# Attention heads: GpSimd splits the last key tile of the transposed exponentials, ScalarE copies it in fp32, and the output sum is made in place

## What is computed

```
x = x + L0_ffn(L0_cond(x))          # an oscillator stepped through time, then a gated MLP with a Hadamard mix
Q, K, V = Wq x, Wk x, Wv x          # per batch b of 8: 16 heads of 16 channels, 512 positions
att = (Q^T K) / sqrt(16) + b0
att = att * m + (1 - m) * -1e30     # m: one mask value per key
att = softmax(att)                  # over 512 keys
y = att V                           # per head 512 x 16
x = x + L1_ffn(y)                   # 8 experts, the top 2 of each position
```

## Time and profile before

| | us |
|---|---|
| median of 3 runs (3069.7 to 3072.78) | 3070.81 |
| the profiled execution | 3071.74 |
| its span | 3070.0 |
| PE busy (41104 matmuls) | 2550.0, 83% |
| DVE busy | 2533.3, 83% |
| ACT busy | 1217.3, 40% |
| POOL busy | 1352.2, 44% |

### The profile page before, as it was taken

One profiled execution on the slowest core, in us unless ns is written; L12 is line 12 of the kernel. 1 busy time (PEld: TensorE's weight loads), 2 busy tenths in 40 slices (PEclk: granted clock), 3 DMA queues, 4 the chain that ended last, 5 costly groups with the idle time before them and its releaser, 6 DMA issues. The chain is left out here.

```text
span 3070.0 us, 116365 instructions
## 1 busy us (share of the span) xinstructions
PE 2550.0 (83%) x41104; PEld 1785.2 (58%) x41104; DVE 2533.3 (83%) x11914; ACT 1217.3 (40%) x4102; POOL 1352.2 (44%) x3951
## 2 busy tenths in 40 slices
PE   4478888888888888888888778888888876999999
PEld 4356666666666666666667446555655552444444
DVE  7989999999999999999997579989999976544545
ACT  3343333333333333333333368778877760000000
POOL 6846566656666566655563323334333335000000
PEclk6599999999999999999999889999999998999999
DMA  4100000000000000000000431110111110000000
GB/s 180 42 19 10 4 10 10 10 3 10 10 10 10 3 10 10 10 7 7 10 10 10 178 91 34 46 47 25 38 47 43 37 63 8 10 17 27 0 27 14
DMA packets 43922, 88.98 MB, mean 29 GB/s; under 512 B 7168, under 2 KB 23808, under 8 KB 41600
## 3 DMA queue, kind: packets, MB, share of 16 engines
q1 hardware_dynamic: 36336, 63.11, 6.4%
q10 hardware_dynamic: 4752, 10.49, 0.9%
q0 software_dynamic: 2304, 8.39, 0.8%
HBM read 65.18 MB, written 16.78 MB: 27 GB/s over the span
## 5 line engine op out<-in xcount | busy, mean ns | idle before, releaser
L228 PE MATMUL rest<-Tl,CW 128*128 128x56 f16 x16384 | 618.1, 190 | 315.4 <-DVE Tl L494 314.9
L228 PEld LDWEIGHTS rest<-Tl,CW 128*128 128x128 f16 x16384 | 502.6, 97 | 561.2 <-DVE Tl L494 557.5
L347 ACT ACTIVATE Tf<-X 128x32 f32<-128x32 f32 x768 | 176.2, 229 | 779.2 <-DVE X L538 779.2
L1114 DVE CUSTOM_DVE_ANT_0 negL<-Lps,negC 128x512 f32<-128x512 f32 x512 | 339.7, 682 | 43.9 <-PE Lps L1022 42.7
L1032 PE MATMUL Tps<-idS,Pr 128*128 128x128 f32 x2048 | 292.3, 288 | 93.9 <-ACT Pr L1084 87.9
L1134 DVE TENSOR_TENSOR PT<-Tps,PT 128x512 f16<-128x512 f32 x512 | 348.4, 681 | 22.8 <-ACT PT L1091 21.2
L1084 ACT ACTIVATE Pr<-negL,nM 128x512 f32<-128x512 f32 x512 | 358.2, 729 | 17.2 <-DVE nM L1114 16.9
L1091 ACT ACTIVATE PT<-Tps 128x512 f16<-128x512 f32 x512 | 293.0, 597 | 139.9 <-PE Tps L1032 139.8
L625 POOL TENSOR_TENSOR G<-X,Dr 128x32 f32<-128x32 f32 x768 | 207.1, 270 | 300.2 <-DVE X L499 273.2
L1032 PEld LDWEIGHTS Tps<-idS,Pr 128*128 128x128 f32 x2048 | 229.9, 145 | 185.1 <-DVE PT L1134 131.5
L217 PE MATMUL main<-Th,CW 128*128 128x56 f16 x8224 | 264.2, 189 | 10.3 <-DVE CW L450 10.3
(11 more groups left out here) (133 smaller groups left out, 5159.1 us busy)
## 6 DMA issues: line engine op xcount, KB each, us to landing
stage<-w_up SPq DMA_DIRECT2D x8, 1024.0 KB, 4.6
qk<-qkp ACTq DMA_DIRECT2D x32, 256.0 KB, 2.4
QR<-qk SPq DMA_DIRECT2D x128, 64.0 KB, 2.2
KR<-qk SPq DMA_DIRECT2D x128, 64.0 KB, 3.2
wstage<-moe_up POOLq DMA_DIRECT2D x16, 512.0 KB, 5.6
W2m<-w_down SPq DMA_DIRECT2D x1, 4096.0 KB, 13.4
stage<-x_tb SPq DMA_DIRECT2D x16, 256.0 KB, 2.6
x<-stage SPq DMA_DIRECT2D x16, 256.0 KB, 2.1
```

Of the source, the lines that this page charges most:

```text
L228: last = pe.matmul(rest[:, m], CW[:, 0, k, m * P:(m + 1) * P], Tl[:, k:k + 1, :].to_broadcast([P, REP, B]), start=(m == 0 and k == 0), sto ...
L1114: dve.tensor_tensor_reduce(out=negL[:, qt, :], in0=Lps[qt % 2][:, :], in1=negC[:], scale=1.0, scalar=3.0e38, op0=ALU.add, op1=ALU.min, acc ...
```

## The change

Of the four key tiles, three are treated as before. For tile 3 (`KD`), ScalarE copies `Tps[3]` in fp32 into a new buffer `last_f` (two deep, by head), and GpSimd makes both halves from it in a new function `split_last`: a copy into the high half and a subtract into the low half. `split_last` of head h-1 stands in GpSimd's step behind `split_output` of head h-3. VectorE has three low halves to make per head instead of four, and its row sums now stand ahead of the last of them. TensorE's transposes of tile 3 wait for ScalarE's copy (`s_cp`) of the head before, its values wait also for GpSimd (`s_pl`), and ScalarE's copy of tile 3 waits for the split of two heads ago. Apart from that the buffer `yf` is gone: `split_output` writes its sum over the first part in `yn`, and the normalization waits for the sum of a head one later than before.

```diff
--- before.py
+++ after.py
@@ -854,8 +854,8 @@
         Pr = sb("Pr", [P, 2, DC, D])
         PT = sb("PT", [P, 2, 2, DC, D], F16)
         yn = sb("yn", [P, 4, DC, 2 * DH])
-        yf = sb("yf", [P, DC, DH])
         wstage = sb("wstage", [P, 2, 1024])
+        last_f = sb("last_f", [P, 2, D])
         Lps = [ctx.enter_context(nc.psum_tensor(f"Lps{i}", [P, 512], F32)) for i in range(2)]
         Tps = [ctx.enter_context(nc.psum_tensor(f"Tps{i}", [P, 512], F32)) for i in range(4)]
         Ops = [ctx.enter_context(nc.psum_tensor(f"Ops{i}", [P, DC, 128], F32)) for i in range(2)]
@@ -865,12 +865,14 @@
             sem("s_L"), sem("s_neg"), sem("s_exp"), sem("s_T"), sem("s_hi"), sem("s_lo"), sem("s_pv"),
             sem("s_norm"), sem("s_y"), sem("s_ri"))
         s_yh, in_moe, moe_t, moe_hi, moe_lo = sem("s_yh"), [sem("in_moe0"), sem("in_moe1")], sem("moe_t"), sem("moe_hi"), sem("moe_lo")
+        s_cp, s_ph, s_pl = sem("s_cp"), sem("s_ph"), sem("s_pl")
         halt = sem("halt2")
         block = ctx.enter_context(nc.Block())
 
 
         AHEAD = 8
         COPIES = 3
+        KD = DC - 1
 
         def load_qk(sp, b, half):
 
@@ -924,6 +926,7 @@
         @block.gpsimd
         def _(pool):
             pool.sem_inc(s_y, AHEAD)
+            pool.sem_inc(s_pl, AHEAD)
             pool.wait_ge(in_id, 32)
             pool.sem_inc(halt, 1)
 
@@ -975,17 +978,29 @@
 
                 i = b * NH + h
                 cols = slice(h * DH, (h + 1) * DH)
+                yf = yn[:, h % 4, :, 0:DH]
                 pool.wait_ge(s_norm, i + 1 + AHEAD)
                 pool.sem_inc(halt, 1)
-                pool.tensor_tensor(yf[:], yn[:, h % 4, :, 0:DH], yn[:, h % 4, :, DH:2 * DH], ALU.add).then_inc(s_y, 1)
+                pool.tensor_tensor(yf, yf, yn[:, h % 4, :, DH:2 * DH], ALU.add).then_inc(s_y, 1)
                 pool.wait_ge(s_y, i + 1 + AHEAD)
                 pool.sem_inc(halt, 1)
-                pool.tensor_copy(YH[:, b, :, cols], yf[:]).then_inc(s_yh, 1)
+                pool.tensor_copy(YH[:, b, :, cols], yf).then_inc(s_yh, 1)
                 pool.wait_ge(s_yh, 2 * i + 1)
                 pool.sem_inc(halt, 1)
-                pool.tensor_tensor(YL[:, b, :, cols], yf[:], YH[:, b, :, cols], ALU.subtract).then_inc(s_yh, 1)
+                pool.tensor_tensor(YL[:, b, :, cols], yf, YH[:, b, :, cols], ALU.subtract).then_inc(s_yh, 1)
                 pool.wait_ge(s_yh, 2 * i + 2)
                 pool.sem_inc(halt, 1)
+
+            def split_last(b, h):
+
+                i = b * NH + h
+                pool.wait_ge(s_cp, i + 1 + AHEAD)
+                pool.sem_inc(halt, 1)
+                pool.tensor_copy(PT[:, h % 2, 0, KD, :], last_f[:, h % 2]).then_inc(s_ph, 1)
+                pool.wait_ge(s_ph, i + 1)
+                pool.sem_inc(halt, 1)
+                pool.tensor_tensor(PT[:, h % 2, 1, KD, :], last_f[:, h % 2], PT[:, h % 2, 0, KD, :],
+                                   ALU.subtract).then_inc(s_pl, 1)
 
             def step(b, h):
                 real = exists(b, h, 0)
@@ -995,6 +1010,8 @@
                     load_weights(b)
                 if exists(b, h, 3):
                     split_output(*before(b, h, 3))
+                if exists(b, h, 1):
+                    split_last(*before(b, h, 1))
                 if not real:
                     return
                 if h in (4, 8):
@@ -1027,14 +1044,18 @@
                 if kc == 0:
                     pe.wait_ge(s_exp, i * DC + DC + AHEAD)
 
-                pe.wait_ge(s_lo, DC * i + kc - DC + 1 + AHEAD)
+                if kc < KD:
+                    pe.wait_ge(s_lo, KD * i + kc - KD + 1 + AHEAD)
+                else:
+                    pe.wait_ge(s_cp, i + AHEAD)
                 for qt in range(DC):
                     last = pe.transpose(Tps[kc][:, qt * P:(qt + 1) * P], Pr[:, h % 2, qt, kc * P:(kc + 1) * P], idS[:])
                 last.then_inc(s_T, 1)
 
             def values(b, h):
                 i = b * NH + h
-                pe.wait_ge(s_lo, DC * i + DC + AHEAD)
+                pe.wait_ge(s_lo, KD * i + KD + AHEAD)
+                pe.wait_ge(s_pl, i + 1 + AHEAD)
                 pe.wait_ge(s_norm, i - 1 + AHEAD)
                 for qt in range(DC):
 
@@ -1074,6 +1095,7 @@
         def _(act):
             act.sem_inc(s_exp, AHEAD)
             act.sem_inc(s_hi, AHEAD)
+            act.sem_inc(s_cp, AHEAD)
 
             def exps(b, h, qt):
                 i = b * NH + h
@@ -1088,7 +1110,11 @@
                 i = b * NH + h
                 act.wait_ge(s_T, i * DC + kc + 1 + AHEAD)
                 act.wait_ge(s_pv, i - 1 + AHEAD)
-                act.activation(PT[:, h % 2, 0, kc, :], Tps[kc][:, :], ACT.Copy).then_inc(s_hi, 1)
+                if kc < KD:
+                    act.activation(PT[:, h % 2, 0, kc, :], Tps[kc][:, :], ACT.Copy).then_inc(s_hi, 1)
+                else:
+                    act.wait_ge(s_pl, i - 1 + AHEAD)
+                    act.activation(last_f[:, h % 2], Tps[kc][:, :], ACT.Copy).then_inc(s_cp, 1)
 
             def step(b, h):
                 for qt, kcs in ((0, (0, 1)), (1, (2,)), (2, (3,)), (3, ())):
@@ -1123,26 +1149,26 @@
 
             def normalize(b, h):
                 i = b * NH + h
-                dve.wait_ge(s_y, i - 3 + AHEAD)
+                dve.wait_ge(s_y, i - 2 + AHEAD)
                 dve.wait_ge(s_ri, i + 1)
                 dve.tensor_tensor(yn[:, h % 4], Ops[h % 2][:, :, 0:2 * DH],
                                   ri[:].unsqueeze(2).to_broadcast([P, DC, 2 * DH]), ALU.mult).then_inc(s_norm, 1)
 
             def transposed_low(b, h, kc):
 
-                dve.wait_ge(s_hi, (b * NH + h) * DC + kc + 1 + AHEAD)
+                dve.wait_ge(s_hi, (b * NH + h) * KD + kc + 1 + AHEAD)
                 dve.tensor_tensor(PT[:, h % 2, 1, kc, :], Tps[kc][:, :], PT[:, h % 2, 0, kc, :], ALU.subtract).then_inc(s_lo, 1)
 
             def step(b, h):
                 if h == 0 and exists(b, h, 0):
                     dve.wait_ge(negc_ok, b + 2)
                     dve.sem_inc(halt, 1)
-                for qt, kcs in ((0, ()), (1, (0,)), (2, (1,)), (3, (2, 3))):
+                for qt, kcs in ((0, ()), (1, (0,)), (2, (1,)), (3, (2,))):
                     if exists(b, h, 0):
                         negate_and_max(b, h, qt)
+                    if qt == DC - 1 and exists(b, h, 2):
+                        invert_sums(*before(b, h, 2))
                     for kc in kcs:
-                        if kc == DC - 1 and exists(b, h, 2):
-                            invert_sums(*before(b, h, 2))
                         if exists(b, h, 1):
                             transposed_low(*before(b, h, 1), kc)
                 if exists(b, h, 2):
```

## The result

The changed kernel takes 3076.66 us (median of 13 executions, 3073.85 to 3081.14); the kernel before, run beside it, 3070.81 (13 executions). The ratio is 1.0023 with an interval of 1.0014 to 1.0031, so + 7.1 us (4.3 to 9.5); the two medians alone lie 5.9 apart. The profiled execution took 3076.66, its span is 3074.2; the forecast was 3074.5, as "Forecast (3072.5 to 3078)".

The account below looks back on a forecast made before the run. The prediction took a closed ring of ScalarE and TensorE, 5.39 us per head step, to bound the kernel. Terms 2.1 + 0.6 + 1.0 = + 3.7 on the kernel before, 3070.81, gave 3074.5; range 3069 to 3086.

Parts of the forecast that it names:

- The ring: Head step in the loop: eight ScalarE instructions, 4.49 us, plus 0.90 waiting for TensorE's transposes make 5.39, without VectorE.
- VectorE's relief at 0: Attention heads: one subtract of four less per head takes 77 us from VectorE, none from the step; gain 0.
- VectorE is the bound after all: Rival: if the row of 131.5 us idle behind VectorE is right, loop steps shrink, - 19 us, near 3052; chance 0.07.
- The fp32 copy at 0: ScalarE's last copy per head: writing fp32 takes the same 597 ns as f16, and its new wait is met; 0.
- The sum in place at 0: GpSimd's output sum: removes a buffer and no instruction, and the normalization's earlier need is still met; 0.
- GpSimd's price: GpSimd's added copy and subtract per head: together 2.04 us; its busy time up by 128 x (0.61 + 1.16) = 227 us.
- The deadline: Tile 3's split before the value matmuls: due 4.03 us after the copy, 4.4 behind mask terms; 0.4 late, costing nothing.
- The mask sum at the first boundary: First batch boundary: mask sum behind the new split starts 2.2 us later, delaying VectorE and the transposes; + 2.1, once.
- The back-edges, 0.6: Six loop back-edges: later mask sum mostly hidden in TensorE's pause; 0.1 us taken for each, 0.6 in all.
- GpSimd comes late at the edges: Rival: GpSimd's branch starts only after the subtract, each of six edges 2.3 us late, + 16.7 in all; chance 0.22.
- The way out, + 1.0: Last head: GpSimd's split ends at 2513.9, where VectorE's subtract ended at 2512.96; + 1.0 us.
- GpSimd and VectorE disturbing each other: Rival: GpSimd's work 19% slower beside VectorE, 92.6 of 86.2 us per batch, + 51 us, near 3122; chance 0.04.

Follow-up runs that it names:

- experiment 1: Kernel before, with VectorE's low half of key tile 3 left out and made by nobody: 3073.04 us, ratio 1.0004.
- experiment 2: ScalarE's copy of tile 3 cut to 16 of 512 columns, in the kernel before (3041.81 us), in that of experiment 1 (3029.42) and in the changed kernel (3057.24).
- experiments 2 and 6: Experiment 2, and the kernel before with ScalarE's copy of tile 3 behind the fourth exponential and VectorE's low half one step later: 3046.69 us, ratio 0.9909.
- experiment 5: Kernel before, with only the output sum made in place: 3072.95 us, ratio 0.9996.
- experiment 4: Changed kernel again (+ 5.5 us); mask sum ahead of the split (+ 5.2, again + 3.7); mask terms also spread (+ 0.3); last head also on VectorE (+ 0.3).
- the mask sum first: Changed kernel, with GpSimd's mask sum of the next batch ahead of the split in step 15: + 5.2 us against the kernel before, again + 3.7.
- the changed kernel with the short copy: Changed kernel, with ScalarE's copy of tile 3 cut to 16 of 512 columns: 3057.24 us, ratio 0.9946 to the kernel before.
- experiment 3: Changed kernel, with GpSimd's split copying 256 columns once more and waiting for that, 0.56 us more per head: 3141.29 us, ratio 1.0233.

## Why the prediction was right, point by point

- *The ring, and VectorE's relief at 0: right.* 5.39 became 5.40, experiment 1 shows the relief alone at no gain, experiment 2 that ScalarE's list is what the time follows. The rival "VectorE is the bound after all" (3052) falls with them, and the reading of the 131.5 us as misnamed is shown. Small parts were off. Of VectorE's new idle time about half, not a third, is the wait for the value matmuls (0.36 in the step above where 0.2 was expected). And VectorE's own work is 5.10 per step, the value at which experiments 2 and 6 stop with no idle time on VectorE, not 5.19.
- *The fp32 copy at 0: right*, 0.60 and 0.61. *The sum in place at 0: right*, experiment 5.
- *GpSimd's price: right.* 0.61 and 1.16; the busy time rose by 218 us, not 227, because the page counts once the time in which an instruction starts under the one before it; the single durations add up to 227 more.
- *The deadline: the moment right, what hides it mis-sized.* The split of the step behind the mask terms ended 4.26 after the copy (2046.37 to 2050.63), 4.4 was predicted. The step of the prediction that failed is "these have a pause of 0.87, so 0.4 costs nothing". The late start costs 0.4 and then another 0.6 in the first two groups of value matmuls (from their start to the next scores it is 1.89, otherwise 1.27). Together 1.0 is more than the cover of 0.87, so each of seven steps is about 0.15 longer: + 1.1 where 0 stood. The eighth, in the unrolled first batch, is a test of this: its values start 0.35 late, the first groups behind them take the usual time, and its step stays at 5.24. Spreading the mask terms takes the + 1.1 away (experiment 4).
- *The mask sum at the first boundary: the mechanism right, the term + 2.1 mis-sized.* The mask sum and VectorE came when they should: VectorE starts 3.83 after ScalarE's copy, 3.97 was predicted. But a pause of 2.15 on TensorE was taken to cost 2.15. It also cost the clock: the step with the pause is 2.8 longer (8.16), the next still 1.1 (6.53), + 3.9 in all. Both are gone with the mask sum first (10.79). That the rest is the clock's is shown by the changed kernel with the short copy (experiment 2), whose pause at this boundary met no fall of the clock:

```profile
1880.66 0.39 PE L1041 MATMUL Lps<-KR,QR 64*128 64x512 f16 x1 [2.00 <-DVE nM L1143]
1880.97 1.09 PE L1054 MATMUL Tps<-idS,Pr 128*128 128x128 f32 x8
```

```profile
1880.60:1886.00 5.40, 5.11 (x54) 3.54 (x55) 5.15 (x14) 4.05 (x8) 2.84 (x5) 1.00 0.37 98
```

There the step is 6.95, 1.97 above its 4.98, and the next is 4.98. So a price of the pause alone, as the + 2.1 was, occurs as well; the prediction named no second price for a fall of the clock.
- *The back-edges, 0.6: nothing seen.* The mask sum starts 1.11 after the subtract, as any GpSimd instruction in a row does, at each of the six edges, and is done well before VectorE can go. If GpSimd's branch has a price here, all of it lies under the subtract. With that the rival "GpSimd comes late at the edges" falls for this kernel. Its mechanism is real all the same: with 0.56 us more per head the 1.9 to 2.8 of idle time appear at every edge, and the mask sum releases VectorE (experiment 3). Why the changed kernel is spared, no run shows. The Trainium skill, Runtime: NRT & Kernel Launch, Instruction fetch mechanics, lets a taken branch out of the held window wait for its page; TensorE's 3.15 at this edge goes with that, GpSimd's row shows no such wait in the changed kernel, and the 1.9 to 2.8 of experiment 3 go with it.
- *The way out, + 1.0: right*, 6.39 to 7.39.
- *GpSimd and VectorE disturbing each other: did not happen.* The subtract takes 1.160 on the mean of 128, VectorE's 0.69 are as before. The Trainium skill's warning (Perfetto Trace Analysis, Optimizing Scalar/DVE Operations) has no place in this trace.

So the forecast, 2.2 us below the median, owes its nearness to a large term that was right at 0, and to two small ones that were too low by 1.8 and 1.1, with 0.6 too high beside them.

## What to carry to other kernels

Before an engine is relieved, find the closed ring that sets the step: the engine whose instructions and one wait add up to it. A busy share of 83% and a releaser of 131 us pointed at VectorE; a sum of eight ScalarE instructions and 0.90 pointed elsewhere, and an instruction moved into that 0.90 brought 27 us where a quarter of VectorE's subtracts taken away, 62 us of its busy time, brought none.

When work goes to an idle engine, ask what it now stands ahead of in that engine's list and who waits for that, at the boundaries most of all (the first one, the last one, the one that has no pause to hide in). A wait that reaches TensorE can cost more than its length: 3.9 for 2.15 here, 1.97 for 2.00 where the clock stayed up. And an engine that comes late shows costs that were hidden while it was early, as GpSimd's at the back-edges.

## What the hardware showed that was not expected

- A pause of 2.15 us on TensorE, at full clock before, was followed by a granted clock of 0.50 over the next 5.4 us, and cost 3.9 us where the pause alone would be 2.15. In experiment 3 a pause of 1.69 ahead of the values was followed by slow scores too. But a longer pause doesn't always bring it: with 2.00 in the short-copy kernel and 2.10 in the unrolled first batch of experiment 3 (row below) the granted clock stayed at 1.00. What decides, these runs don't show.
- Value matmuls that start late, behind GpSimd's split, take 0.59 and 0.60 for their first two groups of four and then the usual 0.34 and 0.27, at a granted clock of 1.00 in that stretch. The weight loads of the two groups stretch likewise (0.47 and 0.50 against 0.21 and 0.20), in all seven such steps of the loop. Never in the unrolled first batch, though: in experiment 3 its seven late starts, after pauses of 0.27 to 2.10, all have the usual 0.34 and 0.27. So a late release by GpSimd is not enough for it. In the loop of the changed kernel it is there in part behind weight splits as well, where the values start without a pause: up to 0.58 from the first group to the third, usually 0.29. Why, these runs don't show.

```profile
2050.84 0.47 PEld L1065 LDWEIGHTS Ops<-V,PT 128*128 128x128 f16 x4 [0.67 <-issue]
2051.34 0.50 PEld L1069 LDWEIGHTS Ops<-V,PT 128*128 128x128 f16 x4
2051.76 0.22 PEld L1065 LDWEIGHTS Ops<-V,PT 128*128 128x128 f16 x4
```

Experiment 3, first batch:

```profile
1876.24 0.34 PE L1069 MATMUL Ops<-V,PT 128*128 128x99 f16 x4 [2.10 <-issue]
1876.42 0.27 PE L1073 MATMUL Ops<-V,PT 128*128 128x51 f16 x4
```

- GpSimd stood idle for 1.9 to 2.8 us at each back-edge of experiment 3, and not at all at those of the changed kernel.
- The pairs of steps around a back-edge vary by 1.2 to 2.5 us within one execution (13.8 to 16.8 over the kernels compared). With six of them in an execution, that is a part of what hides effects of 1 to 2 us in this kernel.
